# Block-turned loads of x and context, context mask and norm as rows, and one accumulating VectorE operation per head for causal mask, sign and maximum

## The chip, the cores and the metric

The kernel runs on one core of one Trainium2 chip. The metric is the device time of one execution in microseconds (us). All data is fp32 unless said otherwise. The engines are TensorE (PE), ScalarE (ACT), VectorE (DVE), GpSimd (POOL) and SyncE (SP), which here only issues transfers.

## What is computed

The reference chains four blocks over 128 batch rows of 128 x 256. Cut to what matters here:

```python
# block 0: decoder layer, 16 heads of 16, x and context (128, 128, 256)
def _mha(x, kv, Wq, Wk, Wv, mask, causal):
    Q, K, V = (einsum('bsd,hdk->bhsk', t, W) * mask for t, W in ((x, Wq), (kv, Wk), (kv, Wv)))
    energy = einsum('bhsk,bhtk->bhst', Q, K)
    lengths = sum(energy[:, :, 0, :] != 0, axis=-1)      # keys beyond it are masked
    ...                                                  # causal mask for self
    return softmax(energy / sqrt(dk)) @ V * mask
mask0 = 1.0 - all(x == 0, axis=2, keepdims=True)
x1 = layernorm(x + mha(x, x, ..., mask0, causal=True), ln1)
mask1 = 1.0 - all(x1 == 0, axis=2, keepdims=True)
x2 = layernorm(x1 + mha(x1, context, ..., mask1, causal=False), ln2)
x3 = layernorm(x2 + ffn(x2) * mask0, ln3)
# block 1: features = context, query = x3
norm_X = layernorm(context) * n1_w + n1_b;  norm_F = layernorm(x3) * n2_w + n2_b
cross = fc2(gelu(fc1(attention(norm_F, norm_X, norm_X, D ** -0.5))))
norm_cross = layernorm(cross) * n3_w + n3_b
x4 = norm_F + gamma2 * (cross + gamma1 * attention(norm_cross, norm_cross, norm_cross, D ** -0.5))
# block 2
x5 = x4 + softmax(x4 @ context.T) @ context
# block 3: layer norm, 8 heads of 32 on (x5, context), layer norm, projection to u, then
s = silu(s @ A.T) + u_t            # 128 steps in sequence, all batch rows at once
return x6 + states @ C + mod
```

## The kernel before, in words

The 128 batch rows form 64 groups (NG) of G = 2. A group's data is a tile of 128 positions x (2 x 256), called natural, or its transpose of 128 of the 256 features x (2 halves x 256 columns, W), called turned. Ten units carry a group from its input to the store: self_in, self_att, ctx_in, ctx_att (block 0's attentions), ffn, pair (block 1), real (block 2), mix_in, mix_att, mix_out (block 3). After the last group a second part of the program runs the 128 scan steps and writes the output.

Each engine has one list of steps, written out in PROGRAM (lines 139 to 207) as unit.step@lag. The function drive (249 to 260) walks the list once per iteration and runs each step for group i - lag; with a largest lag of 6 there are 70 iterations. An engine works in order, so a step that waits holds up all that stands behind it. The waits are counted semaphores: Steps.done is for a result, Steps.before for a buffer to be free, and BANKS (209 to 223) assigns each matmul result one of eight PSUM banks. At iteration PREPARED (3) each engine also runs a piece of one-time preparation; at MOD_STORED (6) SP stores the rows of mod.

The steps that the change touches:

- self_in.xT, ctx_in.cT, pair.CT and real.ccT on PE turn the natural x, masked context (CB), normalised context (HC) and plain context (CC): four 128x128 matmuls against ident each (L554). ACT copies each result to SBUF (evac, L909; HCT for CT). ctx_in.k and .v, and pair.sc1, mix_in.k and .v, and real.screal consume them.
- ctx_in.amax and keep on DVE (L1198, L1204) find the rows of x1 that aren't all zero; POOL's ctx_in.mask (L1514) multiplies the natural context CB by keep. POOL copies the small keep tiles onward (keep, copies1, copies2), so that the next group may overwrite them.
- lnC: DVE's bn_stats, POOL's power and product give scale and shift per row; ACT's lnC (L988) writes HC from CC; then CT and HCT; DVE's NXT applies n1_w and n1_b out of PSUM.
- self_in.v and ctx_in.v are copied from PSUM by ACT; DVE's valid, copy and vp multiply them by the valid column, which has come from nz, count and spread on DVE and the length matmul on PE.
- ctx_att.x1r on ACT copies x1 (L960), because the next group's ln1 overwrites it.
- self_att.mask.br on DVE adds the causal table to a PSUM tile of four heads (128 x 512, L1120), self_att.max.br takes the negated maximum per head (L1127), and ACT's exp uses it as bias, one piece of 128x128 per head. There are 8 tiles per group.
- softmax_one (pair's two, real's one): maximum (mx), a scaling by -scale (nm), exp with that bias.
- SP's list loads x twice (X for the turn, XR for the residual), context twice (CB, CC), the mod rows, and stores u and the result.

Of the kernel before, what the change touches and what calls it, by code (L numbers as in the profile page):

```python
# [24 lines left out]
G = 2  # L25
# [85 lines left out]
def latest(*counts):  # L111

    high = {}
    for c in counts:
# [26 lines left out]
        ctx_att.scores.10@4 mix_att.scores.00@6 pair.cross@5 ctx_att.values.03@4 ctx_att.values.01@4  # L141
        ctx_att.turn.11@4 ctx_att.values.00@4 ctx_att.values.02@4 ctx_att.turn.12@4 ctx_att.turn.13@4
        ctx_att.turn.10@4 mix_in.k@5 real.ccT@5 ctx_att.values.12@4 ctx_att.values.13@4 ctx_att.values.10@4
        ctx_att.values.11@4 ctx_in.x1T@3 ctx_att.back.0@4 mix_att.turn.02@6 ctx_att.back.1@4 self_att.scores.00@2
        self_att.scores.02@2 self_att.scores.01@2 ctx_in.cT@3 pair.ncT@5 ctx_in.q@3 pair.sc2@5 mix_att.turn.03@6
        ctx_in.k@3 pair.pT2@5 mix_att.turn.00@6 self_att.scores.10@2 self_att.scores.11@2 self_att.scores.03@2
        pair.av@5 mix_att.turn.01@6 self_att.turn.01@2 ffn.x2T@4 mix_att.values.00@6 mix_att.values.03@6
        mix_att.values.01@6 ctx_in.e0@3 mix_att.values.02@6 ffn.fc1@4 self_att.turn.02@2 self_att.turn.00@2
        real.x4T@5 ffn.fc2@4 self_in.len@2 real.screal@5 mix_out.o@6 self_in.xT@1 self_att.turn.03@2
        self_att.turn.11@2 real.pTreal@5 ctx_att.scores.01@3 self_att.scores.13@2 self_att.scores.12@2  # L150
        self_att.values.01@2 self_att.values.02@2 self_att.values.00@2 self_att.values.03@2 real.av@5 ctx_in.v@3
        self_in.k@1 self_att.back.0@2 self_in.q@1 self_att.turn.12@2 self_att.turn.10@2 mix_out.h6T@6
        self_att.turn.13@2 ctx_att.scores.00@3 ctx_att.scores.03@3 ctx_att.scores.02@3 self_in.v@1 ctx_in.len@3
        pair.CT@4 self_att.values.10@2 self_att.values.11@2 self_att.values.13@2 self_att.values.12@2
        ctx_att.scores.11@3 ctx_att.scores.13@3 ctx_att.scores.12@3 real.h5T@5 pair.FT@4 ctx_att.turn.01@3
        mix_in.v@4 pair.sc1@4 self_att.back.1@2 ctx_att.turn.00@3 mix_in.q@5 ctx_att.turn.02@3 ctx_att.turn.03@3
        pair.pT1@4 self_in.e0@1 mix_out.u@6 pair.av1@4
    """,
    "act": """
# [1575 lines left out]
```

## Time and profile before

| | us |
|---|---|
| median of three runs | 4111.22 |
| the runs | 4104.85 to 4113.52 |
| span of the profiled execution | 4106.6 |

The page gives the span of one profiled execution, busy time of each engine in it, and groups of instructions by line, engine and tiles. PE is TensorE's matmuls, PEld its weight loads, which overlap them. A matmul's record overlaps that of the one behind it, so the time that a step takes of an engine is read from its start to the next one's start. Waiting isn't counted as busy.

### The profile page before, as it was taken

Reading aid. Unit: us, or ns where it says so; the run is one execution under the profiler, and the core shown is the slowest. Engines: PE = TensorE matmul, PEld = TensorE weight load, DVE = VectorE, ACT = ScalarE, POOL = GpSimd, SP = SyncE. Lnnn points to the kernel's source line nnn. Section 1 sums busy time; section 2 is a strip of 40 time slices with the busy share of each in tenths; the row PEclk is TensorE's granted clock in tenths of the full one; section 3 lists DMA queues with packets and bytes.
Section 4 is the critical chain, followed back from the end, with each engine's and each line's share of the span. In section 5 each row is a group of like instructions: output and inputs, shape, how many; then the busy total and the mean of one; then the engine's idle time right before and its main releaser. Section 6 shows DMA issues by size and latency. Waiting matters only on the chain. (4 is left out here: it accounts for less than half of the span.)

```text
span 4106.6 us, 111739 instructions
## 1 busy us (share of the span) xinstructions
PE 3913.2 (95%) x37177; PEld 3233.6 (79%) x37177; DVE 3349.2 (82%) x9519; ACT 3547.9 (86%) x8460; POOL 2854.5 (70%) x3172
## 2 busy tenths in 40 slices
PE   6899999999999999999999999999999999999859
PEld 5688888888888888888888888888888888887647
DVE  4788888888888888888888888888888888888635
ACT  4799999999998999999899999989999998999635
POOL 2577777777777777777777777777777777777636
PEclk7999999999999999999999999999999999999969
DMA  3001011011101101110110111011011101100038
GB/s 115 22 29 34 20 31 34 20 34 31 34 20 31 34 21 33 31 34 20 31 34 23 31 31 34 20 31 34 23 32 31 34 20 31 34 24 28 18 80 306
DMA packets 121876, 159.94 MB, mean 39 GB/s; under 512 B 12296, under 2 KB 108450, under 8 KB 116642
## 3 DMA queue, kind: packets, MB, share of 16 engines
q1 hardware_dynamic: 116896, 145.39, 11.5%
q10 hardware_dynamic: 4416, 7.41, 0.5%
q8 instruction: 307, 5.03, 0.5%
q14 instruction: 257, 2.11, 0.2%
HBM read 114.86 MB, written 37.75 MB: 37 GB/s over the span
## 5 line engine op out<-in xcount | busy, mean ns | idle before, releaser
L618 PE MATMUL bank<-ident,prob 128*128 128x128 f32 x5120 | 728.8, 277 | 56.9 <-ACT CR L1005 26.9
L938 ACT ACTIVATE probT<-bank 128x512 f32<-128x512 f32 x1280 | 730.6, 593 | 59.6 <-PE bank L618 56.7
L909 ACT ACTIVATE turned<-bank 128x512 f32<-128x512 f32 x896 | 538.7, 601 | 186.9 <-PE bank L554 177.8
L618 PEld LDWEIGHTS bank<-ident,prob 128*128 128x128 f32 x5120 | 590.9, 142 | 138.4 <-issue 48.8
L1138 DVE TENSOR_REDUCE mx<-bank 128x4 f32<-128x512 f32 x768 | 507.9, 682 | 187.3 <-PE bank L589 184.7
L927 ACT ACTIVATE prob<-prob,mx 128x128 f32<-128x128 f32 x2048 | 650.6, 396 | 4.1 <-DVE mx L1127 4.0
L562 PE MATMUL bank<-turned,shared 128*128 128x256 f32 x2560 | 616.4, 384 | 1.2 <-ACT turned L909 1.1
L1444 POOL TENSOR_TENSOR rs_ln<-ve_ln,half 128x2 f32<-128x2 f32 x320 | 227.3, 710 | 446.8 <-DVE ve_ln L1109 446.8
L1149 DVE TENSOR_TENSOR prob<-bank,mx 128x512 f32<-128x512 f32 x768 | 520.7, 685 | 15.3 <-PE bank L618 1.9
L562 PEld LDWEIGHTS bank<-turned,shared 128*128 128x128 f32 x2560 | 469.8, 191 | 69.0 <-issue 12.3
L919 ACT ACTIVATE prob<-prob 128x512 f32<-128x512 f32 x768 | 475.5, 636 | 13.0 <-DVE prob L1149 12.1
L589 PE MATMUL bank<-shared,turned 32*128 32x256 f32 x4096 | 448.5, 403 | 3.4 <-DVE prob L1120 2.2
L1523 POOL TENSOR_SCALAR shared<-turned,half_of 128x512 f32<-128x512 f32 x256 | 399.7, 1574 | 29.8 <-ACT turned L909 29.7
L1120 DVE TENSOR_TENSOR prob<-bank,causal 128x512 f32<-128x512 f32 x512 | 345.1, 685 | 57.0 <-PE bank L618 47.3
L570 PE MATMUL bank<-shared,turned 128*128 128x256 f32 x1536 | 369.9, 384 | 0.6 <-DVE turned L1256 0.5
L1127 DVE TENSOR_REDUCE mx<-prob 128x4 f32<-128x512 f32 x512 | 347.3, 679 | 16.8
L589 PEld LDWEIGHTS bank<-shared,turned 32*128 32x128 f32 x4096 | 284.7, 185 | 82.6 <-issue 47.2
L570 PEld LDWEIGHTS bank<-shared,turned 128*128 128x128 f32 x1536 | 281.5, 190 | 55.2 <-issue 22.2
L652 PE MATMUL bank<-probT,shared 128*32 128x128 f32 x8192 | 291.7, 278 | 0.9 <-ACT probT L938 0.8
L1458 POOL TENSOR_TENSOR X<-X,row_ln_g 128x512 f32<-128x512 f32 x192 | 245.5, 1279 | 63.2 <-ACT X L988 63.2
L1534 POOL TENSOR_TENSOR prob<-prob,inv 128x512 f32<-128x512 f32 x256 | 263.5, 1040 | 16.7 <-DVE inv L1165 16.7
L652 PEld LDWEIGHTS bank<-probT,shared 128*32 128x32 f32 x8192 | 205.2, 110 | 76.6 <-issue 75.4
(238 smaller groups left out, 9071.8 us busy)
## 6 DMA issues: line engine op xcount, KB each, us to landing
shared<-in_x SPq DMA_DIRECT2D x128, 256.0 KB, 2.9
CB<-in_ctx SPq DMA_DIRECT2D x64, 256.0 KB, 4.0
CC<-in_ctx SPq DMA_DIRECT2D x64, 256.0 KB, 2.7
mod<-mod_rows SPq DMA_DIRECT2D x64, 256.0 KB, 3.8
residual<-X SPq DMA_DIRECT2D x64, 256.0 KB, 3.1
out<-turned SPq DMA_DIRECT2D x16, 1024.0 KB, 4.8
turned<-residual SPq DMA_DIRECT2D x14, 1024.0 KB, 7.1
u_turned<-us SPq DMA_DIRECT2D x124, 32.0 KB, 2.2
```

The costliest lines, as they stand in the source:

```text
L562: last = nc.tensor.matmul(t[:, m * W:(m + 1) * W], w[:, a, m * 128:(m + 1) * 128], src[:, a, :], start=(a == 0), stop=(a == DH - 1))
L570: last = nc.tensor.matmul(t[:, b * D:(b + 1) * D], src[:, a, b * S:(b + 1) * S], w[:, a, :], start=(a == 0), stop=(a == DH - 1))
L589: last = nc.tensor.matmul(t[:, a * W:(a + 1) * W], QT[p][rows_, a, b * S:(b + 1) * S], KEYS[p][rows_, a, :, b * S:(b + 1) * S], start=True ...
L618: last = nc.tensor.transpose(t[:, h * 128:(h + 1) * 128], src[:, h, :], ident[:])
L652: last = nc.tensor.matmul(t[k * 32:(k + 1) * 32, r * 128:(r + 1) * 128], VP[p][:, b, 4 * r + k, :], src[:, k, :], start=True, stop=True)
L909: nc.scalar.activation(dst, banks.of(f"{unit}.{name}")[:, 0:n], ACT.Copy).then_inc(*st["act"].mark(name))
L919: nc.scalar.activation(flat(t), flat(t), ACT.Exp, scale=SCALE[p]).then_inc(*st["act"].mark(f"exp.{b}{r}"))
L927: last = nc.scalar.activation(t[:, h, :], t[:, h, :], ACT.Exp, bias=low[:, h:h + 1], scale=1.0)
L938: nc.scalar.activation(flat(t), banks.of(f"{att}.turn.{b}{r}")[:, :], ACT.Copy).then_inc(*st["act"].mark(f"probT.{b}{r}"))
L1138: nc.vector.tensor_reduce(m[:], banks.of(f"{att}.tile.{b}{r}")[:, :].rearrange("p (h t) -> p h t", h=4), AX, ALU.max)\
L1149: nc.vector.tensor_tensor(t[:], banks.of(f"{att}.tile.{b}{r}")[:, :].rearrange("p (h t) -> p h t", h=4), maxes.of(f"{att}.max.{b}{r}")[:]. ...
L1523: last = nc.gpsimd.tensor_scalar(KEYS[p][:, :, c, :], KT[p][:], half_of[:, c:c + 1], None, ALU.mult)
```

## The change

- x and context are also loaded in blocks: in_blocks issues four DMAs per 256 KB, by an index that swaps 32x32 blocks (runs of 32 elements). A DVE transpose of 128x512, which turns each 32x32 block in place, then gives XT (self_in.xT on DVE) and ccT (ctx_in.cT on DVE, three buffers). The PE steps xT, cT, ccT and CT and the ACT copies behind them go.
- Scaling by position, which in the turned layout is along the row: keep of ctx is stored to HBM (rowout) and loaded back broadcast to all partitions (rowin) as kept_row; lnC's scale and shift likewise as norm_row. POOL computes CBT = ccT * kept_row (mask), HCT = ccT * norm_row 0 (hcs), + norm_row 1 (HCT). ACT's lnC and HCT go; NXT reads HCT in SBUF.
- Causal mask, sign and maximum: per head one tensor_tensor_reduce on DVE writes -(score + causal) and accumulates its minimum; exp has scale -1.
- nz accumulates the count itself; the length matmul takes the count broadcast and the table head_at; valid goes straight into vp's column; vp reads v out of PSUM. nm, count, spread and the ACT copies of v and x1 go, the last by two x1 buffers; keep0 and keep1 get four buffers each in place of POOL's copies.
- New lists and banks, PREPARED 2, MOD_STORED 5; SP's mod load one iteration earlier. The amax of self reads XR.

```diff
-PREPARED, MOD_STORED = 3, 6
+PREPARED, MOD_STORED = 2, 5
...
+    x_q, ctx_q = (t.rearrange("(g b) (k c) (a j i) -> g j c a b k i", b=G, c=32, j=4, i=32) for t in (x_d, ctx_d))
...
+                def in_blocks(t, src, g, here):
+                    v = t[:].rearrange("p b d -> p (b d)").rearrange("p (a b k i) -> p a b k i", a=DH, b=G, i=32)
+                    for j in range(4):
+                        sp.dma_start(v[32 * j:32 * j + 32], src[g, j]).then_inc(here.sem, 16)
...
+                def kept_to(g):
+                    for w in latest(kept_in.before(g), ctx_in["dve"].done("keep", g)):
                         sp.wait_ge(*w)
+                    sp.dma_start(kept_d.rearrange("(b s o) -> s b o", b=G, o=1), keep1[g % 4][:].unsqueeze(2), allow_slow_non_contiguous=True)\
+                        .then_inc(kept_out.sem, 16)
+
+                def kept_from(g):
+                    for w in latest(kept_out.done(g), ctx_in["pool"].before("mask", g)):
+                        sp.wait_ge(*w)
+                    sp.dma_start(kept_row, kept_d.partition_broadcast(128)).then_inc(kept_in.sem, 16)
...
                     def mask_(g):
...
-                        nc.vector.tensor_tensor(t[:], banks.of(f"{att}.tile.{b}{r}")[:, :].rearrange("p (h t) -> p h t", h=4),
-                                                causal[:].unsqueeze(1).to_broadcast([128, 4, 128]), ALU.add).then_inc(*st["dve"].mark(f"mask.{b}{r}"))
-
-                    def low(g):
...
-                        nc.vector.tensor_reduce(m[:], probs.of(f"{att}.mask.{b}{r}")[:], AX, ALU.max, negate=True)\
-                            .then_inc(*st["dve"].mark(f"max.{b}{r}"))
+                        for h in range(4):
+                            last = nc.vector.tensor_tensor_reduce(t[:, h, :], banks.of(f"{att}.tile.{b}{r}")[:, h * 128:(h + 1) * 128], causal[:],
+                                                                  -1.0, 3.0e38, ALU.add, ALU.min, m[:, h:h + 1])
...
+                def x_turned(g):
+                    waits_apart(dve, prep, *latest(x_in.done(g), *(self_in["pe"].before(n, g) for n in "qkv")))
+                    nc.vector.transpose(flat(trn["XT"]), x_blocks.rearrange("p b d -> p (b d)")).then_inc(*self_in["dve"].mark("xT"))
...
                 def mask(g):
 
-                    waits_apart(pool, prep, *latest(ctx_in2.done(g), ctx_in["dve"].done("keep", g)))
-                    for b in range(G):
-                        last = nc.gpsimd.tensor_scalar(nat["CB"][:, b, :], nat["CB"][:, b, :], keep1[0][:, b:b + 1], None, ALU.mult)
-                    last.then_inc(*ctx_in["pool"].mark("mask"))
+                    for w in latest(kept_in.done(g), ctx_in["dve"].done("cT", g), ctx_in["pe"].before("k", g), ctx_in["pe"].before("v", g)):
+                        pool.wait_ge(*w)
+                    nc.gpsimd.tensor_tensor(trn["CBT"][:], ccT[g % 3], kept_row.unsqueeze(1).to_broadcast([128, DH, W]), ALU.mult)\
+                        .then_inc(*ctx_in["pool"].mark("mask"))
```

In PE's new list 17 steps stand between ctx_in.x1T and ctx_in.k:

```
ctx_in.x1T@3 ctx_att.turn.10@4 ctx_att.values.03@4 ctx_att.values.11@4 ctx_att.values.12@4 ctx_att.values.13@4
ctx_att.values.10@4 mix_att.turn.02@6 ctx_att.back.0@4 ctx_att.back.1@4 ctx_in.q@3 pair.ncT@5 self_att.scores.03@2
self_att.scores.01@2 self_att.scores.00@2 mix_att.turn.03@6 pair.sc2@5 mix_att.turn.00@6 ctx_in.k@3
```

SP's new list:

```diff
-        mix_out.load@6 ctx_in.load@3 pair.load@4 self_in.load@0 mix_out.store@6 mix_out.store_u@6 self_att.load@1
+        pair.rowin@4 pair.load@2 self_in.load@0 ctx_in.load@2 ctx_in.rowout@2 mix_out.load@5 mix_out.store@6
+        pair.rowout@3 ctx_in.rowin@2 self_att.load@1 mix_out.store_u@6
```

## Rows read from the trace of the kernel before

**Rows 1.** The page's head: the span and the instructions.

```profile
span 4106.6 us, 111739 instructions
```

**Rows 2.** Line L965 (mix_out.attT, once per group): ns min/median/max, first and last start.

```profile
L965 ACT ACTIVATE turned<-bank x64: 575/598/606, 154.5 to 3916.8; 128x512 f32<-128x512 f32 x64
```

**Rows 3.** Stretch 2000-2060: length, busy PE, PEld, DVE, ACT, POOL, PEclk, DMA, GB/s.

```profile
2000.00:2060.00 60.00, 58.52 (x565) 48.50 (x564) 50.70 (x144) 54.15 (x129) 43.52 (x49) 1.00 0.10 29
```

**Rows 4.** Waits of PE over the whole span: us in total, times, longest.

```profile
PE bank L770 <- ACT y5T L998: 31.0, 64, 1.6
PE bank L618 <- ACT CR L1005: 26.9, 62, 0.5
...
PE bank L618 <- ACT prob L919: 15.4, 64, 1.4
```

**Rows 5.** Timeline of PE: start us, record us, line, result<-operands, matmuls.

```profile
2006.49 0.63 PE L554 MATMUL bank<-ident,HC 128*128 128x128 f32 x4
2007.05 1.08 PE L652 MATMUL bank<-probT,shared 128*32 128x128 f32 x32
...
2027.64 0.60 PE L554 MATMUL bank<-ident,CC 128*128 128x128 f32 x4
2028.17 1.08 PE L652 MATMUL bank<-probT,shared 128*32 128x128 f32 x32
...
2032.60 0.66 PE L554 MATMUL bank<-ident,CB 128*128 128x128 f32 x4
2033.10 0.63 PE L554 MATMUL bank<-ident,NC 128*128 128x128 f32 x4
2033.57 1.89 PE L562 MATMUL bank<-turned,shared 128*128 128x256 f32 x8
...
2051.62 0.60 PE L554 MATMUL bank<-ident,shared 128*128 128x128 f32 x4
2052.06 1.04 PE L618 MATMUL bank<-ident,prob 128*128 128x128 f32 x8
```

**Rows 6.** Groups of ACT by line and shape: busy us, mean ns, idle before.

```profile
L909 ACT ACTIVATE turned<-bank 128x512 f32<-128x512 f32 x896 | 538.7, 601 | 186.9 <-PE bank L554 177.8
...
L988 ACT ACTIVATE HC<-CC,nmr_lnC,rs_lnC 128x256 f32<-128x256 f32 x128 | 70.1, 606 | 0.0
```

**Rows 7.** Timeline of DVE: start us, record us, what.

```profile
2025.74 0.17 DVE L1204 TENSOR_SCALAR keep<-amax_ctx 128x2 f32<-128x2 f32 x1
...
2043.10 0.68 DVE L1120 TENSOR_TENSOR prob<-bank,causal 128x512 f32<-128x512 f32 x1
2043.70 0.67 DVE L1127 TENSOR_REDUCE mx<-prob 128x4 f32<-128x512 f32 x1
2044.29 0.28 DVE L1221 TENSOR_SCALAR nz_ctx<-bank 128x128 f32<-128x128 f32 x1
```

**Rows 8.** Timeline of POOL, with the idle time before it in brackets.

```profile
2023.55 1.29 POOL L1464 TENSOR_TENSOR X<-X,row_ln_b 128x512 f32<-128x512 f32 x1
...
2027.54 1.83 POOL L1514 TENSOR_SCALAR CB<-CB,keep 128x256 f32<-128x256 f32 x2 [1.30 <-issue]
```

**Rows 9.** DMA: queue's packets, MB, share; issues: KB each, us to landing.

```profile
q1 hardware_dynamic: 116896, 145.39, 11.5%
...
shared<-in_x SPq DMA_DIRECT2D x128, 256.0 KB, 2.9
...
mod<-mod_rows SPq DMA_DIRECT2D x64, 256.0 KB, 3.8
...
u_turned<-us SPq DMA_DIRECT2D x124, 32.0 KB, 2.2
```

**Rows 10.** Timeline of SP's queue: start us, us of the issue.

```profile
2021.07 0.47 SPq L497 DMA_DIRECT2D mod<-mod_rows  x1
```

**Rows 11.** Timeline of PE in the first groups: preparation and the next transposes.

```profile
58.15 1.84 PE L818 MATMUL bank<-col_be,w_q 128*128 128x1 f32 x8 [3.45 <-DVE NC L1353]
...
77.58 1.09 PE L554 MATMUL bank<-ident,X 128*128 128x128 f32 x4 [0.56 <-issue]
```

More of the change, by code:

```diff
@@ L140 @@
     "pe": """
[L141 to L155, printed above, removed]
@@ new lines @@
+        mix_att.turn.03@6 pair.sc2@5 mix_att.turn.00@6 ctx_in.k@3 pair.pT2@5 self_att.scores.10@2
+        self_att.scores.02@2 self_att.scores.11@2 mix_att.turn.01@6 pair.av@5 self_att.turn.01@2 self_in.len@2
+        ffn.x2T@4 mix_att.values.03@6 mix_att.values.00@6 mix_att.values.02@6 ctx_in.e0@3 mix_att.values.01@6
+        self_att.turn.00@2 ffn.fc1@4 self_in.v@2 ffn.fc2@4 real.x4T@5 self_att.turn.03@2 self_att.turn.02@2
+        ctx_in.len@3 real.screal@5 mix_out.o@6 self_att.scores.12@2 ctx_att.scores.01@3 self_att.scores.13@2
@@ L162 @@
-        ctx_att.probT.03@4 ctx_att.probT.02@4 pair.gelu@5 self_att.ln1@3 pair.cross@5 ctx_att.exp.13@4
-        ctx_att.exp.10@4 ctx_att.probT.11@4 mix_att.exp.02@6 ctx_att.probT.13@4 ctx_att.probT.12@4
-        ctx_att.probT.10@4 mix_att.exp.03@6 ctx_att.outT.0@4 pair.lnN@5 ctx_att.outT.1@4 real.ccT@5 mix_att.exp.00@6
-        ctx_in.x1T@3 ctx_in.cT@3 mix_att.exp.01@6 pair.ncT@5 mix_att.probT.02@6 self_att.exp.01@2 ctx_in.q@3
-        pair.exp2@5 ctx_att.ln2@4 pair.pT2@5 mix_att.probT.03@6 ctx_in.k@3 mix_att.probT.00@6 self_att.exp.00@2
@@ L199 @@
[L199 to L202 removed]
+        self_att.add@3 pair.lnCpow@4 self_att.ln1pow@3 self_att.ln1nmr@3 ffn.biased@4 real.x5b@6 pair.lnCnmr@4
@@ new lines @@
+        self_att.ln1gain@3 self_att.ln1@3 pair.lnNpow@5 pair.lnNnmr@5 mix_att.part.02@6 pair.lnNgain@5
+        pair.lnN@5 mix_att.part.03@6 ctx_att.add@4 mix_att.part.00@6 ctx_in.mask@3 ctx_att.ln2pow@4
+        ctx_att.ln2nmr@4 mix_att.part.01@6 ctx_att.ln2gain@4 ctx_att.ln2@4 pair.hcs@4 pair.skip@5 pair.gam2@5
+        ffn.x2b@4 pair.x4@5 ctx_in.keys@3 ffn.ln3pow@4 ffn.ln3nmr@4 pair.HCT@4 ffn.ln3gain@4 ffn.ln3@4
+        mix_out.ln6pow@6 mix_out.ln6nmr@6 pair.lnFpow@4 pair.lnFnmr@4 real.ln5pow@5 real.ln5nmr@5 pair.lnFgain@4
@@ new lines @@
+    mix_in.k:0 ctx_att.out.1:0 ctx_in.x1T:6 ctx_att.back.0:1 mix_att.turn.02:2 ctx_att.back.1:7
+    self_att.tile.00:1 self_att.tile.02:5 self_att.tile.01:5 pair.ncT:2 ctx_in.q:6 pair.sc2:4 mix_att.turn.03:3
+    ctx_in.k:3 pair.pT2:4 mix_att.turn.00:6 self_att.tile.10:2 self_att.tile.11:0 self_att.tile.03:7 pair.av:7
+    mix_att.turn.01:1 self_att.turn.01:4 ffn.x2T:5 mix_att.out.0:3 ctx_in.e0:6 ffn.fc1:5 self_att.turn.02:2
+    self_att.turn.00:7 real.x4T:4 ffn.fc2:6 self_in.len:1 self_in.v:3 real.screal:0 mix_out.o:5
@@ L223 @@
+    ctx_att.turn.02:6 ctx_att.turn.03:0 pair.pT1:2 self_in.e0:5 mix_out.u:2 pair.av1:7
 """.split())
```

410 lines of the change are left out of this document (200 added, 210 removed).

## The prediction

> **What bounds the kernel now.** I read the head of the page first: the span is 4106.6 us [rows 1]. Then a view of how one work step recurs, the starts of the 64 mix_out.attT copies: 154.5 to 3916.8 us, so 63 periods of 59.72 us, with about 155 us before and 190 us behind them [rows 2]. Nearly all of the time is 64 repetitions of one pattern, and each microsecond saved or added per group is worth 63 to 64 us. The stretch 2000 to 2060 us, one period, shows which engine is full: TensorE (PE) busy 58.52 of 60.00 us, ScalarE (ACT) 54.15, VectorE (DVE) 50.70, GpSimd (POOL) 43.52, DMA a tenth, TensorE's granted clock 1.00 throughout [rows 3]. So PE's in-order list sets the period; its idle is 1.48 us. The table of waits says what that idle is: the three entries that recur some 62 to 64 times are all waits on ACT, 31.0 + 26.9 + 15.4 = 73.3 us [rows 4]. What counts of an edit is therefore PE time removed, or a wait that PE gains.
>
> Against its own time: the span is 4106.6, the median of the runs 4111.2, so 4.6 lies around the span, and I add it at the end.
>
> **The change, part by part.**
>
> **Four transposing steps leave PE** (xT, cT, CT, ccT: four 128x128 matmuls each). A pipelined step is priced from its start to the start of the step behind it, not by its record: HC 2006.49 to 2007.05 is 0.56, CC 2027.64 to 2028.17 is 0.53, CB 2032.60 to 2033.10 is 0.50, shared (the self input) 2051.62 to 2052.06 is 0.44 [rows 5]. The sum is 2.03 us per group, 64 x 2.03 = **-130 us**. PE gets nothing in return; the length matmul only changes its operands.
>
> **ACT** loses the copies of these four (CT's is HCT), of the two v, the x1r copy (all 128x512, 0.60) and two lnC pieces of 0.61 [rows 6]: 7 x 0.60 + 2 x 0.61 = 5.4 us, from 54.15 to about 48.7. ACT isn't the bound, so this pays only where PE waits on ACT, at most 73 us [rows 4]. They stand behind pair's gelu, the copies of pair.cross and one exponential; those operations stay, though order and banks around them are new, and an ACT that is a tenth emptier reaches them somewhat earlier. I take a fifth, **-16 us** (0 to -73).
>
> **DVE, mask and maximum.** Per self tile a 128x512 addition and a 128x512 reduction go, 0.60 + 0.59 from start to start, eight tiles: -9.5 us. In come 32 accumulating operations of 128x128, each on a PSUM tile and the causal table. The trace has none of that kind. The nearest row is nz, 128x128 out of PSUM: 0.28; the floor is the smallest operation, 0.17, the ceiling nz plus one such for writing the accumulator, 0.45 [rows 7]. I take 0.28: 9.0 us (5.4 to 14.4).
>
> The Trainium skill, "VectorE: DVE Perf Modes", section "The TRN2 errata — SBUF-src ops pay a fixed extra latency per instruction", speaks against this edit: many small tiles each pay the fixed part, so a tile should have 512 elements or more. Its measured form for fp32 tensor_tensor, (N+151)/0.96 ns, gives as an estimate 0.29 us for 128 columns and 0.69 for 512 (the trace has 0.68 for the mask). By it, four small ones take 1.16 us instead of 2 x 0.69 = 1.38: cutting the tile costs three fixed parts but saves one whole pass. The sum would be 9.3 instead of 9.0. The accumulator write isn't in that form.
>
> **DVE, the rest.** Two transposes of 128x512 come in; no such row exists, and at the 0.60 of a 128x512 pass [rows 7] they are 1.2 us (half to double: 0.6 to 2.4). Out go two counts (taken like nz), and seven small steps (two spreads, three nm, two copies) at 0.17: 1.75, less 0.08 of overlap each, 1.05. DVE becomes 50.70 - 9.5 + 9.0 + 1.2 - 1.05 = 50.4 (46 to 57), still 7 us below PE's 56.5. **0.**
>
> **POOL** loses the mask of CB (1.83 for its two pieces) and gets three 128x512 passes at 1.29 (mask, hcs, HCT) [rows 8]: 43.5 - 1.8 + 3.9 = 45.6, uncounted that four tiny keep copies go. **0** by load.
>
> **Loads in blocks.** x and context are now read in runs of 128 bytes: 2048 runs per 256 KB load, 128 on each of 16 DMA engines. The page's queue has 116896 packets in 11.5% of 16 engines' span, 0.115 x 16 x 4106.6 / 116896 = 65 ns each [rows 9], so 128 x 65 ns = 8.3 us per load against 2.9 now. Each is issued an iteration before its use, with some 20 us or more in hand. That slack is the cover; gone, it would cost what rival E says. **0.** Six more issues for the blocks and five for the rows below, at 0.47 [rows 10], are 5.2 us more on SP's queue, whose transfers take a tenth of the engines' time [rows 3].
>
> **The mask row, the new wait.** keep of ctx no longer scales CB on POOL directly. It goes to HBM, comes back broadcast, POOL multiplies ccT by it, and ctx_in.k on PE waits for that. From ln1's end: amax about 0.7 and keep 0.2 [rows 7]; a store, landing like that of u in 2.2; meanwhile SP, where the row's return stands behind the mod load, the result store and two norm rows, issues these four at 0.47 (1.9, beside the 2.2; the waits among them, for mod and lnCnmr on POOL, stand early enough in POOL's list); the return like the mod rows' broadcast, 3.8 [rows 9, 10]; POOL 1.3 [rows 8]. Together 0.9 + 2.2 + 3.8 + 1.3 = 8.2, with a wait or two between, 8.2 to 8.7. The cover is what PE does between x1T, which starts from the same ln1, and k: five values steps (4 take 1.08: 0.27 each), four turns (two take 1.04: 0.52 each), two backs and ncT (0.5 each), q (1.9) [rows 5], together 1.35 + 2.1 + 1.5 + 1.9 = 6.8, and three score tiles and sc2 behind their own inputs, which bring it to 9 if those inputs are there. So k comes between 0 and 2 us late, 0 to 126 us in all. If it is late, all of PE behind it is: pT2, the self scores, then DVE's masks. I take 0, as the score tiles stand ahead of k in the list and the pipeline can slide the other units into the gap; the bound stays in the range. POOL too stands at the mask until the row is there; ln2 queues behind it, and ffn.x2T for that, some 8 steps after k.
>
> The norm rows for HCT take the same way, but are needed half a period later. **0.**
>
> **Prologue.** PE's preparation (from 58.15) moves one iteration forward. In before it lies 19.4 us ahead of the next transposes of groups [rows 11]. Moved forward it can stand in an otherwise empty iteration (0) or hold the first groups up by as much as it lasts (19.4). I take **+8**, since its loads come no earlier. The last stage with its scan isn't changed: 0.
>
> **Sum:** 4106.6 - 130 - 16 + 8 = 3968.6; with 4.6 around the span **3973 us**, the period 59.72 - 2.03 - 0.25 = 57.4.
>
> **The rivals.**
>
> C, *PE's waits on ACT vanish altogether*: ACT and DVE have gained over 5 and 0.3 us, and the order is new. For it: all recurrent waits are on ACT [rows 4]. Against: each is a short chain (score, exponential, turn) whose own latency doesn't shrink. 4106.6 - 130 - 73 + 8 + 4.6 = 3916.
>
> A, *the mask row through HBM comes late*, the one that ends slower. Place: ctx_in.k on PE, behind ctx_in.mask on POOL, behind the row's return on SP. Price: 63 us per microsecond late. It decides from (4111 - 3973) / 63 = 2.2 us per group. At 3 us, the store and the return each some 1.5 us slower than their rows, 3973 + 189 = 4162. For it: 4-byte elements, a store whose like isn't in the trace, and a queue in order. Against: 0.5 to 2 us is what the rows give at most.
>
> B, *DVE becomes the bound*: with 0.45 for each accumulating operation, DVE works 55.8 us; if half of the 9.3 us stay that it idles now [rows 3], its period is 60.4, 4106.6 + 63 x 0.7 + 8 + 4.6 = 4163. Against: the nz row.
>
> D, *another chain through the in-order lists sets the period*, and PE's freed time turns into waits: about 4115. Against: PE is busy 97.5% of the period, so no other chain is known to be as long.
>
> E, *the block loads don't arrive in time.* Two loads of 128 packets per engine fill a group's 57 us from 0.22 us per packet on, 3.4 times the mean. At 19 times the 2.9 us of the plain load, 55 us each, the period would be 110 us, 7000 us in all. The factor is that of the Trainium skill, same page, section "The three transpose paths", a trap: a plain DMA that transposes by strides is 19 times slower than the transposing DMA path when the destination's innermost stride is large. Here the innermost 32 elements are contiguous on both sides, so it hardly applies; no row shows such a load.
>
> **How the numbers follow.** The forecast has 0.62 (its own range 3925 to 4060: relief beyond a fifth below, k late by up to 1.4 us above), C 0.19, A 0.08, D 0.05, B 0.04, E 0.02. The range 3890 to 4085 takes in C with a prologue that costs nothing, and a k late by up to 1.8 us. About 0.2% is what a measurement of this kernel can tell from no change. Faster: forecast and C, 0.81; same: D, 0.05; slower: A, B, E, 0.14.
>
> **What would show it.** Right: PE shows no transposes of HC, CC, CB and x; the period is near 57.4; k's idle before the step is below 0.5 us, and the recurrent waits are still on ACT. Wrong: an idle of 2 us or more before ctx_in.k, released by POOL (A); an accumulating operation of 0.45 or more with DVE busy 95% of the period (B); DVE's transposes waiting on a DMA (E); PE's busy time near 56 in a period still near 59.7 (D). The accumulating operation's mean, the transposes' mean and the landing time of the kept row show the three estimates directly.

## The result, and the profile after

The changed kernel takes **4578.81 us** in the median (4577.64 to 4583.64), the kernel before 4109.74 in the runs beside it: a ratio of 1.1138 (95% interval 1.112 to 1.1157). The forecast was 3973 in a range of 3890 to 4085, so both the size and the sign were wrong. What happened is rival A, the late mask row, but two and a half times as large as that rival made it (469 us against 189), and with a second loss that no case had.

The head of the page after, span and busy time of each engine (before: [rows 1]):

```profile
span 4577.3 us, 111103 instructions
PE 3924.9 (86%) x36153; PEld 3193.7 (70%) x36153; DVE 3181.0 (69%) x12272; ACT 3268.7 (71%) x7884; POOL 2931.5 (64%) x2980
```

The table of PE's waits (us in total, times, longest) has one new entry that is larger than all of [rows 4] together:

```profile
PE bank L597 <- POOL turned L1500: 433.7, 64, 12.7
```

L597 is the projection step, L1500 ctx_in.mask on POOL. So ctx_in.k waits in every group, 433.7 / 64 = 6.8 us. The view of L1500 itself names who POOL waited for, with total and times:

```profile
  DMA shared<-kept_rows: 466.0, 64
```

That is the row's return. One group, on the timelines of SP's queue, POOL and PE (start us, record us, line, operation, idle before and its releaser in brackets):

```profile
2064.09 0.37 SPq L507 DMA_DIRECT2D kept_rows<-keep  x1
...
2065.55 0.41 SPq L519 DMA_DIRECT2D norm_rows<-rs_lnC  x1
2066.00 0.52 SPq L519 DMA_DIRECT2D norm_rows<-nmr_lnC  x1
2071.56 0.33 SPq L513 DMA_DIRECT2D shared<-kept_rows  x1
...
2078.44 1.26 POOL L1500 TENSOR_TENSOR turned<-shared 128x512 f32<-128x512 f32 x1 [5.97 <-DMA shared<-kept_rows]
...
2079.84 3.75 PE L597 MATMUL bank<-turned,shared 128*128 128x256 f32 x8 [5.71 <-POOL turned L1500]
```

The store of keep is issued at 2064.09. SP issues the four transfers ahead of the row's return, as the prediction had it, in 2.0 us, then stands until 2071.56, since the store has not landed. The return takes another 6.9 us to the mask's start. The step of k then costs 3.75 us where the row of before has 1.89 [rows 5]. The reason is in the granted clock. Three stretches of this group (length; busy PE, PEld, DVE, ACT, POOL with their counts; PEclk; DMA; GB/s):

```profile
2072.00:2080.00 8.00, 2.29 (x20) 1.94 (x18) 5.00 (x36) 1.58 (x6) 2.03 (x3) 0.81 0.25 69
2080.00:2085.00 5.00, 5.00 (x23) 3.55 (x23) 0.00 (x0) 2.02 (x6) 4.55 (x6) 0.62 0.11 35
2085.00:2120.00 35.00, 35.00 (x317) 30.14 (x315) 27.44 (x112) 30.21 (x79) 25.11 (x25) 1.00 0.13 25
```

PE works 2.29 of 8 us, the clock drops from its upper level (1.00, 2.4 GHz) towards the lower one (half, 1.2 GHz), and the 5 us behind the wait run at a mean of 0.62. In the 35 us behind them the clock is whole and PE is full, as in [rows 3].

The parts of the change that the prediction priced with bounds, from DVE's groups (busy us, mean ns | idle before), beside its timeline of one self tile:

```profile
L1134 DVE CUSTOM_DVE_ANT_0 prob<-bank,causal 128x128 f32<-128x128 f32 x2048 | 459.6, 285 | 573.6 <-PE bank L653 543.1 <-PE bank L624 29.6 <-issue 0.8
L1134 DVE DVE_READ_ACCUMULATOR2_ANT mx<- 128x1 f32 x2048 | 169.9, 83 | 0.0
...
L1202 DVE STREAM_TRANSPOSE turned<-shared 128x512 f32<-128x512 f32 x64 | 44.5, 695 | 4.4 <-DMA shared<-in_x 4.4
```

```profile
2087.40 0.28 DVE L1134 CUSTOM_DVE_ANT_0 prob<-bank,causal 128x128 f32<-128x128 f32 x1
2087.61 0.08 DVE L1134 DVE_READ_ACCUMULATOR2_ANT mx<- 128x1 f32 x1
2087.61 0.29 DVE L1134 CUSTOM_DVE_ANT_0 prob<-bank,causal 128x128 f32<-128x128 f32 x1
...
2088.24 0.28 DVE L1245 TENSOR_SCALAR shared<-bank,iota 128x32 f32<-128x32 f32 x1
```

An accumulating operation has a record of 0.28 us and a readout of 0.08, but the next one starts 0.21 behind it: a tile's four take 2088.24 - 2087.40 = 0.84 us. The transposes take 0.70.

The block loads, from the DMA issues (packets, KB each, median us from issue to landing):

```profile
shared<-in_x SPq DMA_DIRECT2D x256, 64.0 KB, 2.5
CB<-in_ctx SPq DMA_DIRECT2D x256, 64.0 KB, 2.4
```

### The profile page after: what moved, and what is told of

Its sections match the earlier page's. It is cut to its first block and busy times, and to the rows that moved or that the text cites. A ratio compares the mean times of both kernels' runs of the same rounds, so it can differ in the third digit from the quotient of the medians.

```text
span 4577.3 us, 111103 instructions
## 1 busy us (share of the span) xinstructions
PE 3924.9 (86%) x36153; PEld 3193.7 (70%) x36153; DVE 3181.0 (69%) x12272; ACT 3268.7 (71%) x7884; POOL 2931.5 (64%) x2980
## 5 line engine op out<-in xcount | busy, mean ns | idle before, releaser
L597 PE MATMUL bank<-turned,shared 128*128 128x256 f32 x2560 | 732.3, 437 | 454.3 <-POOL turned L1500 433.7
L597 PEld LDWEIGHTS bank<-turned,shared 128*128 128x128 f32 x2560 | 536.4, 219 | 552.7 <-issue 468.4
L1134 DVE CUSTOM_DVE_ANT_0 prob<-bank,causal 128x128 f32<-128x128 f32 x2048 | 459.6, 285 | 573.6 <-PE bank L653 543.1
L653 PE MATMUL bank<-ident,prob 128*128 128x128 f32 x5120 | 770.3, 280 | 38.7 <-ACT probT L964 25.8
L653 PEld LDWEIGHTS bank<-ident,prob 128*128 128x128 f32 x5120 | 579.3, 142 | 195.6 <-issue 73.5
L935 ACT ACTIVATE turned<-bank 128x512 f32<-128x512 f32 x704 | 412.9, 594 | 216.1 <-PE bank L589 174.1
L1005 ACT ACTIVATE X<-Z,nmr_ln,rs_ln 128x256 f32<-128x256 f32 x192 | 104.8, 592 | 418.6 <-POOL nmr_ln L1449 417.8
L1500 POOL TENSOR_TENSOR turned<-shared 128x512 f32<-128x512 f32 x64 | 81.3, 1270 | 466.0 <-DMA shared<-kept_rows 466.0
L605 PE MATMUL bank<-shared,turned 128*128 128x256 f32 x1536 | 354.4, 380 | 2.1 <-DVE turned L1261 2.1
L1459 POOL TENSOR_TENSOR X<-X,row_ln_g 128x512 f32<-128x512 f32 x160 | 203.3, 1270 | 116.5 <-ACT X L1005 116.4
```

Of the source, the lines that this page charges most:

```text
L597: last = nc.tensor.matmul(t[:, m * W:(m + 1) * W], w[:, a, m * 128:(m + 1) * 128], src[:, a, :], start=(a == 0), stop=(a == DH - 1))
L605: last = nc.tensor.matmul(t[:, b * D:(b + 1) * D], src[:, a, b * S:(b + 1) * S], w[:, a, :], start=(a == 0), stop=(a == DH - 1))
L653: last = nc.tensor.transpose(t[:, h * 128:(h + 1) * 128], src[:, h, :], ident[:])
L935: nc.scalar.activation(dst, banks.of(f"{unit}.{name}")[:, 0:n], ACT.Copy, scale=scale).then_inc(*st["act"].mark(name))
L1134: last = nc.vector.tensor_tensor_reduce(t[:, h, :], banks.of(f"{att}.tile.{b}{r}")[:, h * 128:(h + 1) * 128], causal[:], -1.0, 3.0e38, ALU ...
```

## The experiments

Two theories at the start. The **late row**: the mask row, with the clock that its wait costs, is the whole loss, and the rest of the sum stands. The **new order**: the lists stall one another, and the wait at k is only the place where it shows. Each kernel below is the changed one with the edit named.

### The mask row left out

```diff
-        ... ctx_in.load@2 ctx_in.rowout@2 mix_out.load@5 ... pair.rowout@3 ctx_in.rowin@2 self_att.load@1 ...
+        ... ctx_in.load@2 mix_out.load@5 ... pair.rowout@3 self_att.load@1 ...
-   nc.gpsimd.tensor_tensor(trn["CBT"][:], ccT[g % 3], kept_row.unsqueeze(1)..., ALU.mult)
+   nc.gpsimd.tensor_tensor(trn["CBT"][:], ccT[g % 3], ones_row[:].unsqueeze(1)..., ALU.mult)
```

> Left out: the context mask. POOL multiplies the context by a row of ones written once, and keep of ctx no longer goes to HBM and back; all else is as in the changed kernel. Theory L (the late mask row is the whole of the loss): PE's 434 us of waits at ctx_in.k go, and with them the slow clock behind each, which is about 142 us (PE busy 3924.9 us where 3913.2 less the removed 130 would be 3783): 4577 - 434 - 142 = about 4000 us, PE busy near 3790, granted clock 1.00 in mid-kernel. Theory O (the new order of the lists, or DVE, is a bound of its own behind the row): 4060 to 4115, with waits of PE on DVE or ACT of 2 us or more per group.

Measured: 4109.52 us, a ratio to the kernel before of 0.9992 (0.9983 to 1.0002). The spans, 4577.3 - 4108.6, differ by **468.7 us**. By the pages, PE's idle time falls from 4577.3 - 3924.9 = 652.4 to 292.6 us, so 359.8 of it was waiting, and PE's busy time falls by 3924.9 - 3816.0 = 108.9 for the same 36153 matmuls: the lowered clock. By the trace's record of the granted clock, PE is busy at half clock for 355.9 us in the changed kernel and for 157.1 us here; at whole clock half of the difference, 99 us, would not have been spent. But the kernel is then only level with the one before, 136 us above the forecast. The late row isn't the whole loss.

The head of its page, its largest recurrent wait of PE, and the starts of successive u steps on DVE's timeline:

```profile
span 4108.6 us, 110850 instructions
PE 3816.0 (93%) x36153; PEld 3131.2 (76%) x36153; DVE 3217.6 (78%) x12273; ACT 3269.6 (80%) x7884; POOL 2935.3 (71%) x2980
```

```profile
PE bank L701 <- ACT outT L980: 55.4, 31, 3.7
```

```profile
653.50 0.31 DVE L1340 TENSOR_SCALAR us<-bank,u_b 128x128 f32<-128x128 f32 x1
...
712.37 0.31 DVE L1340 TENSOR_SCALAR us<-bank,u_b 128x128 f32<-128x128 f32 x1
...
769.77 0.31 DVE L1340 TENSOR_SCALAR us<-bank,u_b 128x128 f32<-128x128 f32 x1
...
832.84 0.31 DVE L1340 TENSOR_SCALAR us<-bank,u_b 128x128 f32<-128x128 f32 x1
```

The periods are 58.87, 57.40 and 63.07 us. In the middle of the kernel before they lie between 59.4 and 60.3 us; here some groups lose 1.5 to 6 us and others nothing. The time is the one that the new order was expected to give, but its waits of 2 us per group aren't there: 55.4 us over 64 groups are 0.9.

### The mask row by PE instead of HBM

Two matmuls of keep, broadcast along the columns, with the identity put the row in a PSUM bank; DVE multiplies ccT by it. The computation is whole.

```diff
+   for b in range(G):
+       last = nc.tensor.matmul(t[:, b * S:(b + 1) * S], keep1[g % 4][:, b:b + 1].to_broadcast([128, 128]), ident[:], ...)
...
+   nc.vector.tensor_tensor(trn["CBT"][:], ccT[g % 3], banks.of("ctx_in.row")[:, 0:W].unsqueeze(1)..., ALU.mult)
```

> The whole computation; the mask row is made on the chip instead of through HBM: two 128x128 matmuls of keep (broadcast over the stationary columns) against ident give the row in PSUM on all partitions, DVE multiplies ccT by it (128x512), and POOL's mask pass and both transfers of the row go. PE gains about 0.25 us per group, DVE one pass of 0.69 at a place behind norm.1. Theory L: as row_const plus 16 us of PE, 4010 to 4030. Theory O: 4075 to 4130. If DVE's step at that place holds up what is behind it, PE shows waits on DVE at ctx_in.k or at the self scores' turns.

Measured: 4120.54 us; 1.0017 (1.0005 to 1.0029). A row that never leaves the core costs some 11 us more than no row at all, and the same 136 us and more remain: they don't hang on the mask.

### The return directly behind its store

```diff
-        ... ctx_in.load@2 ctx_in.rowout@2 mix_out.load@5 mix_out.store@6 pair.rowout@3 ctx_in.rowin@2 ...
+        ... ctx_in.load@2 ctx_in.rowout@2 ctx_in.rowin@2 mix_out.load@5 mix_out.store@6 pair.rowout@3 ...
```

> Only SP's list differs: the return of the mask row stands directly behind its store, ahead of the mod load, the result store and the two norm rows. In the changed kernel the store takes 8.7 us from issue to the return's issue, the return 6.8 to POOL's pass. Theory E (256 elements of 4 bytes make the store slow by themselves): the store stays above 7 us, since the first group had 7.3 with neither mod nor result store in flight; the return falls to about 4, as it is no longer behind the norm rows' 512 elements; PE waits some 3 us instead of 7: about 4320 us. Theory T (the traffic between makes it slow): store 2 to 4 us, return 4, no wait at k worth naming: about 4000 to 4030.

Measured: 4686.19 us; 1.1398 (1.1371 to 1.1426). It was expected near 4320, so this is a miss, but it tells two things. With nothing issued behind the store, it still took 8.24 us in the median from its issue to the return's, against 8.62 in the changed kernel: what makes it slow isn't the traffic issued behind it. And while the return itself came faster (5.1 us in the mean to the mask's start, where it was 6.8), the norm rows are now issued later, and POOL stands for them:

```profile
PE bank L597 <- POOL turned L1500: 305.0, 64, 8.9
PE bank L589 <- POOL X L1552: 155.2, 62, 5.2
```

```profile
POOL turned L1507 <- DMA shared<-norm_rows: 389.2, 63, 8.1
POOL turned L1500 <- DMA shared<-kept_rows: 336.0, 64, 14.9
```

The first fence is PE's waits, the second POOL's. The wait at k shrinks by 129 us, a new one of 155 comes up at the transposing of x4 (L1552). The norm rows, "needed half a period later", have no such slack once SP's queue holds them back. Most of the miss is again the clock: against the changed kernel PE is idle for only 27 us more (4693.6 - 4014.0 = 679.6 against 652.4) but busy for 89 us more, and busy at half clock for 521.1 us instead of 355.9, which is worth 83 of them.

### The mask row stored in runs of 128 bytes

keep is 128 x 2; turned in 32x32 blocks by DVE (0.2 us), its values lie along the free axis, and 8 runs of 128 bytes replace 256 elements of 4 bytes. The turn is a step of its own on DVE, behind keep. SP's order is the changed kernel's.

```diff
-   sp.dma_start(kept_d.rearrange("(b s o) -> s b o", b=G, o=1), keep1[g % 4][:].unsqueeze(2), allow_slow_non_contiguous=True)
+   nc.vector.transpose(keep1_t[:], keep1_w[g % 4][:])
+   for b in range(G):
+       sp.dma_start(kept_d.rearrange("(b j c) -> b j c", b=G, c=32)[b], keep1_t[b:128:32, :])
```

> Only the form of the store differs: DVE turns the two keep columns in 32x32 blocks (one more instruction of some 0.2 us), and two transfers store 8 runs of 128 bytes instead of 256 elements of 4 bytes; SP's list is as in the changed kernel. Theory E: from the store's issue to the return's issue 2.5 to 4 us instead of 8.7; the return stays near 6.8 behind the norm rows' stores; PE waits 1 to 3 us: 4080 to 4250. Theory T: 8 us or more as before, about 4570.

Measured: 4452.76 us; 1.0831 (1.0809 to 1.0852). SP's queue in one group:

```profile
2061.83 1.14 SPq L511 DMA_DIRECT2D kept_rows<-keep_t  x2
...
2064.48 0.51 SPq L522 DMA_DIRECT2D norm_rows<-nmr_lnC  x1
2065.09 0.49 SPq L516 DMA_DIRECT2D shared<-kept_rows  x1
...
2074.35 0.34 SPq L528 DMA_DIRECT2D shared<-norm_rows  x1
```

In the same order beside the same traffic, SP issues the return at once behind the norm rows: the store's two halves have landed by then, 3.26 us behind the issue of the first (2065.09 - 2061.83) and, in the median over the groups, 2.66 behind that of the second, where it was 8.62; in SP's waits there is no entry for this store any more. **The store's 8.6 us are its 256 elements** (the turned row also lies in 8 partitions instead of 128; the two aren't told apart). But the return now takes 9.7 us to the mask in the mean instead of 6.8, with the norm rows' 512 elements ahead of it, and PE still waits 304.6 us at k. That these elements are the reason shows further down: with both rows in runs the return takes 3.7.

### Both rows left out

The scaling and addition of the norm rows go against a row of ones too, so the computation lacks mask and normalisation; the POOL passes stay.

```diff
-   nc.gpsimd.tensor_tensor(trn["HCT"][:], ccT[g % 3], norm_row[:, 0, :].unsqueeze(1)..., ALU.mult)
+   nc.gpsimd.tensor_tensor(trn["HCT"][:], ccT[g % 3], ones_row[:].unsqueeze(1)..., ALU.mult)
-   nc.gpsimd.tensor_tensor(trn["HCT"][:], trn["HCT"][:], norm_row[:, 1, :].unsqueeze(1)..., ALU.add)
+   nc.gpsimd.tensor_tensor(trn["HCT"][:], trn["HCT"][:], ones_row[:].unsqueeze(1)..., ALU.add)
```

> Left out: the context mask and the norm of the context (both rows are ones, written once), so that no row goes through HBM. row_const still had the norm rows. There the period, seen between the u steps, swings from 57.1 to 63.5 us; the short ones are the 57.4 that was forecast, the long ones have one stall of up to 3.8 us at PE's back.1, in which PE, ACT, DVE and POOL stand together while an instruction packet of 8 KB takes 3.8 us on its DMA engine; 30 of 367 such packets take over 2 us, in the kernel before none. Theory I (the norm rows' 512 elements of 4 bytes hold the DMA engines for some 10 us per group, and the engines' instructions come late behind them): without them no packet over 2 us, the period 57.4 throughout, 64 x 1.7 = about 110 us less than row_const's 4109: about 4000. Theory D (the new lists' own order makes the swing, instruction packets are a companion): the swing stays, 4080 to 4110.

Measured: 3988.13 us; 0.9706 (0.969 to 0.9722): **121.4 us** below the kernel without the mask row (118 by the two ratios to the kernel before), 15 above the forecast. The head of its page:

```profile
span 3985.3 us, 110468 instructions
PE 3770.2 (95%) x36153; PEld 3099.6 (78%) x36153; DVE 3206.3 (80%) x12273; ACT 3260.5 (82%) x7884; POOL 2930.6 (74%) x2980
```

The spans differ by 4108.6 - 3985.3 = 123.3 us: 292.6 - 215.1 = 77.5 are idle time of PE, 66.5 of them before the matmuls of one line, L701, and 3816.0 - 3770.2 = 45.8 are slower matmuls (busy at half clock for 157.1 us with the norm rows, for 65.3 without). Its u steps:

```profile
631.99 0.31 DVE L1340 TENSOR_SCALAR us<-bank,u_b 128x128 f32<-128x128 f32 x1
...
689.57 0.31 DVE L1340 TENSOR_SCALAR us<-bank,u_b 128x128 f32<-128x128 f32 x1
...
746.96 0.31 DVE L1340 TENSOR_SCALAR us<-bank,u_b 128x128 f32<-128x128 f32 x1
```

57.58 and 57.39: steady, at the forecast's 57.4. So the norm rows cost some 2 us per group, although POOL's waits in the kernel without the mask row have no entry for them. Where, is seen in that kernel in a group that lost time (timelines of PE, ACT and DVE):

```profile
784.15 1.12 PE L701 MATMUL bank<-ident,outT 128*128 128x128 f32 x4 [3.48 <-ACT outT L980]
783.50 0.60 ACT L980 ACTIVATE outT<-bank 128x512 f32<-128x512 f32 x1 [3.32 <-remote]
783.55 0.26 DVE L1185 RECIPROCAL recip_ctx<-bank 128x16 f32<-128x16 f32 x1 [2.60 <-remote]
```

PE, ACT and DVE stand together, and ACT and DVE for "remote", which is no engine of the core. The DMA queues between 779 and 785 us (packets, MB, share of 16 engines):

```profile
q1 hardware_dynamic: 207, 0.24, 40.2%
q14 instruction: 1, 0.01, 3.9%
```

One packet of instructions held its DMA engine for 0.039 x 16 x 6 = 3.7 us. Counted over the instruction packets of 8 and 16 KB between 1000 and 3500 us: over 2 us took none of 362 in the kernel before (longest 1.5), 30 of 367 without the mask row (longest 8.3), none of 375 without both rows. So the elements reach past their own transfer: with them, packets of other queues come late.

That the late instructions make the stalls doesn't follow, though. Of the first 58 periods of the kernel without the mask row, the 29 with an instruction packet of over 2 us and the 29 without one both take 59.3 us in the mean. Of the 26 times between 600 and 3500 us that PE is idle for over 0.8 us, 13 have an instruction packet of over 1 us under way, as in the group above, and 13 have none. What they share is place and time: 24 stand before L701, and 25 begin between the issue of the norm rows' store and that of their return; without both rows there is no such idle time at all. The stalls come with the elements, then; by what way isn't shown.

### Both rows in runs of 128 bytes

The edit of the mask row, and the same for the norm rows: rs and nmr of lnC side by side in one tile, turned by DVE, 16 runs instead of 512 elements. The computation is whole.

```diff
+   rs["lnC"] = lnc_w[:, 0:G]
+   nmr["lnC"] = lnc_w[:, G:2 * G]
+   nc.vector.transpose(lnc_t[:], lnc_w[:])
-   sp.dma_start(norm_d[k].rearrange("(b s o) -> s b o", b=G, o=1), t[:].unsqueeze(2), allow_slow_non_contiguous=True)
+   sp.dma_start(norm_d[k].rearrange("(b j c) -> b j c", b=G, c=32)[b], lnc_t[G * k + b:128:32, :])
```

> The whole computation. Both rows still go through HBM, in SP's order of the changed kernel, but DVE first turns keep and the norm's columns in 32x32 blocks, and the stores are runs of 128 bytes: 8 runs for the mask, 16 for the norm rows, in place of 768 elements of 4 bytes per group. In row_wide (mask alone) the store fell from 8.7 to 2.7 us, but the return grew to 9.8 behind the norm rows' elements. Theory I with E (elements of 4 bytes are the whole cost): store 2.7, return about 4.5, pass 1.3 = 8.5 after the store's issue, inside the cover of 16.7 - 6.8 = 9.9; PE waits under 1 us at ctx_in.k; about 4000 to 4040. If the round trip stays late for another reason: a wait of 3 us or more, 4200.

Measured: **3999.58 us; 0.9732 (0.9712 to 0.9751)**, and in a second set of runs:

> rows_wide again, as the base of the two kernels beside it, and for its interval: 3999.6 us before, 3990 to 4010 expected.

4004.15 us; 0.9737 (0.9721 to 0.9753). This beats both kernels: 2.6% under the one before, 12.5% under the changed one. The profile of the second set (span 4000.7 us): busy times from the page, PE's largest recurrent wait, SP's queue, and the step of k:

```profile
PE 3792.6 (95%) x36153; PEld 3099.2 (77%) x36153; DVE 3228.7 (81%) x12405; ACT 3270.7 (82%) x7884; POOL 2933.2 (73%) x2980
```

```profile
PE bank L659 <- ACT probT L970: 26.6, 63, 0.7
```

```profile
2027.14 1.14 SPq L514 DMA_DIRECT2D kept_rows<-keep_t  x2
...
2031.49 0.38 SPq L519 DMA_DIRECT2D shared<-kept_rows  x1
...
2084.58 1.14 SPq L514 DMA_DIRECT2D kept_rows<-keep_t  x2
```

```profile
2094.22 1.89 PE L603 MATMUL bank<-turned,shared 128*128 128x256 f32 x8
```

The wait at k is gone (4.4 us in the whole span), k is back at 1.89 us, the period is 57.44, and no instruction packet of 380 takes over 2 us (longest 1.9). The transposes and POOL's mask are all still there, so the new order isn't the cause: with its DMAs in other packets, the same order reaches the forecast's period.

### The mask by PE, the norm rows in runs; the scan's loads moved

The two matmuls of above together with the 16 runs:

> The whole computation: the mask row by PE and DVE as in row_pe, the norm rows through HBM in runs of 128 bytes as in rows_wide. row_pe's mid-kernel period was within 0.1 us of row_const's. Theory I: no instruction packet over 2 us, period near 57.5, about 4005 to 4020. Theory D: 4090 to 4120 as row_pe.

Measured: 4011.33 us; 0.976 (0.9741 to 0.978), which the intervals don't tell apart from the mask row in runs through HBM. And that kernel with the last stage's early loads issued behind the result store of the last group but one instead of ahead of it:

```diff
-                    if g == NG - 1:
-                        scan_early()
...
+                    if g == NG - 2:
+                        scan_early()
```

> pe_wide with one more edit: the early loads for the scan (u and residual, 4 MB and more) are issued behind the second-last group's result store instead of ahead of it. In row_const the store of that group was issued at 3936, right behind those loads, and DVE's res of the last group waited 44 us for it; in the kernel before the store came 37 us after the loads. Expected from this: the last interval between u steps from 62.5 to about 27 as before, 35 us less than pe_wide: 3970 to 3985, where the forecast for the change stood. If the loads' lateness then shows at the scan's start, 10 to 20 us of it come back.

Measured: 4007.53 us; 0.9749 (0.9733 to 0.9766), no measurable gain. In the changed kernel, and in those without rows or with both in runs, DVE stands once for the residual near the end, 44.0 to 44.2 us (here without both rows: waits of DVE); the table of the kernel before has no such entry:

```profile
DVE X L1334 <- DMA residual<-X: 44.1, 1, 44.1
```

With the loads moved, PE stands at the start of the scan instead (waits of PE):

```profile
PE bank L1646 <- POOL Z L1662: 33.6, 1, 33.6
```

So the lateness has moved to another wait of the last stage and isn't gone. What would take it away isn't shown.

### The old mask and maximum, everything else as in the best version

The maximum is a step of its own again, directly behind the addition.

```diff
-   for h in range(4):
-       last = nc.vector.tensor_tensor_reduce(t[:, h, :], ..., causal[:], -1.0, 3.0e38, ALU.add, ALU.min, m[:, h:h + 1])
+   nc.vector.tensor_tensor(t[:], ..., causal[:].unsqueeze(1).to_broadcast([128, 4, 128]), ALU.add)
+   nc.vector.tensor_reduce(m[:], probs.of(f"{att}.mask.{b}{r}")[:], AX, ALU.max, negate=True)
```

> rows_wide with one part of the change undone: mask and maximum of a self tile again by a 128x512 addition and a 128x512 reduction on DVE, exp with scale 1. In the trace of the changed kernel four accumulating operations start 0.21 us apart, 0.83 per tile where the two old ones took 1.19, so DVE gets 8 x 0.36 = 2.9 us more per group, some 53 of 57.5. Theory S (as forecast: DVE's time is hidden, the edit is worth nothing): 3990 to 4010. Theory F (the tile's latency between scores and exp is on the path): up to 64 x 2.9 = 186 us more, 4050 to 4190.

Measured: 4054.21 us; 0.9861 (0.9845 to 0.9877), **50 us** more than the 4004.15 beside it. A recurrent wait of PE that the best version doesn't have, and DVE's group of the mask:

```profile
PE bank L595 <- DVE prob L1138: 31.7, 62, 0.5
```

```profile
L1138 DVE TENSOR_TENSOR prob<-bank,causal 128x512 f32<-128x512 f32 x512 | 347.8, 679 | 5.9 <-PE bank L630 5.9
```

A transposing step (L595) waits once per group for a bank that DVE's mask has yet to read out. DVE is nowhere the bound by load, 84% of this span. The addition by itself (0.68) isn't longer than the four accumulating operations (0.84), but with the reduction of one tile ahead of the addition of the next, banks come free later: two tiles in a row start at 2003.41 and 2004.80, 1.39 us apart, where the kernel before needs 1.19 for the pair. The steps stand in the best version's order, not in the old kernel's, so 50 us is what the edit is worth in this order. By the pages 31.4 of the 50.3 us between the spans are idle time of PE, and 18.9 are busy time for the same matmuls at the same mean clock (0.979); why these take longer is open.

### Four transposing steps of PE done twice

Of x2, NF, NC and x4, 16 matmuls more per group, in the best version: the opposite of the change's main term.

```diff
+   for _ in range(2 if any(src is nat[n] for n in ("X2", "NF", "NC", "X4")) else 1):
        for a in range(DH):
```

> rows_wide with PE work put back: four of the transposing steps that are left (x2T, FT, ncT, x4T) do their four matmuls twice into the same bank, 16 matmuls of 0.11 us more per group, as many as the change took away, with no wait or copy added. Theory P (PE's start-to-start work sets the period, as the sum has it): 64 x 1.76 = 113 us more, 4105 to 4120. Theory C (a chain through ACT and DVE sets it, PE has slack): under 50 us more.

Measured: 4106.02 us; 0.9983 (0.9974 to 0.9993): **102 us** more, of 113 expected. Time put on PE costs 0.9 of its price here; that time taken away is worth as much is inferred from it, not measured.

## Why the prediction was wrong, by its steps

| step | forecast | measured |
|---|---|---|
| four transposing steps leave PE | -130 us | 102 of 113 us for four others put back |
| ACT's relief | -16 | recurrent waits on ACT 73.3 to 26.6 in the best version |
| DVE's mask and maximum | 0 | about -50, in the new order |
| block loads | 0 | 0 (DVE waits once, 4.4 us) |
| prologue | +8 | +11 in the best version |
| last stage | 0 | about +36 in the best version |
| norm rows | 0 | **+121**, measured without the mask row |
| mask row | 0, up to 126 | **+469**, measured beside the norm rows |

**The mask row: the right chain, two terms too small.** The prediction made the chain behind keep 2.2 + 3.8 + 1.3 = 7.3 us. It is 16.7 in the mean. "A store, landing like that of u in 2.2" is the first step that failed: 8.62 in the median, at least 7.29. The row that I took is a store of 32 KB in runs [rows 9]; its 2.2 us say nothing of 256 elements of 4 bytes, and I named these elements in rival A without bounding them. "The return like the mod rows' broadcast, 3.8" is the second: 6.77 in the mean, as it stands behind the norm rows' elements. The cover was slightly larger than taken: 16.7 - 6.8 = 9.9 behind keep, for 6.8 to 9 from x1T on. POOL's pass (1.26, taken 1.29) was right. Against the cover as measured, the true store alone would have made k 4 us late, both 7.

**The price of lateness was too small too.** "63 us per microsecond late" counts only the wait. PE's 6.8 us of standing take the clock along: 359.8 us of idle time and 108.9 us of slower matmuls. Here the clock is a third of the wait on top.

**The norm rows: "0" by slack.** The slack was there for the data; yet with the elements under way PE, ACT and DVE stood together in many groups, at a step that has no need of the rows. The prediction looked at who waits for the rows, not at what else goes on while they are stored. That the 121 us are idle time and slow matmuls behind the stalls at one step is measured (77.5 + 45.8 between the spans), and so is that they go when the rows go in runs. Late instruction packets go with the elements too (13 of 325 over 2 us in the changed kernel, 16 of 338 with the mask row alone in runs; none with both rows in runs or left out), but groups that have them lose no more time than groups that don't (59.3 us a period either way). By what way the elements make the engines stand stays open.

**The main term was about right.** With the elements gone, the period is 57.4 as forecast. The best version's span can be put together from the forecast: the 64 u steps lie 116 us closer together than before. That is 152 us less in the repeating part (forecast 130 + 16 = 146), and 36 us more in the last interval (26.9 to 62.6). The first u step comes 11 us later (forecast 8). Together 106 us, and 4106.6 - 4000.7 is 105.9. But single terms offset each other in the 152: by the run with steps doubled the four steps are worth about 130 x 102 / 113 = 117, by the run with the old mask DVE's edit 50, together 167 without ACT's share. What takes the difference back, perhaps POOL's and SP's added work, stays open.

**DVE: "0" because it isn't the bound.** The size was slightly wrong (0.84 us per tile where 4 x 0.28 = 1.12 was taken, against 1.19 of the old pair). The reason for nothing was wrong: an engine 7 us below the bound still decides when a bank comes free for PE. The Trainium skill, "VectorE: DVE Perf Modes", section "The TRN2 errata — SBUF-src ops pay a fixed extra latency per instruction", would have had four small tiles pay their fixed part four times; the trace shows the next one starting 0.21 us behind the last, 0.08 less than the estimate of 0.29 by the page's form, so a part of it overlaps here.

**The last stage: "isn't changed: 0".** Its code isn't, but its first loads are issued among the last groups by SP's list, which is new. How they could be hidden stays open.

**The rivals.** A was the mechanism with a chance of 0.08; its "3 us late, 4162" should have had 7 us and the clock. B and E are refuted: DVE is 81% busy in the best version, and a block load's 64 KB quarter lands in 2.4 to 2.5 us. E's 55 us also multiplied the plain load by a factor that the prediction itself quotes against the transposing path. C's vanishing waits came in part, without the gain. D's 4115 is close to what the kernels without the mask row took (4109.52 and 4120.54), but not by its mechanism: the same lists reach 57.4 us once the elements are gone. The ledger from forecast to result is 3973 + 469 (mask row and clock) + 121 (norm rows) + 15 (the rest as of the run without both rows) = 4578, by its making.

The shares in it depend on the order in which the rows are mended, since the norm rows' elements also hold up the mask row's return. Taken out of the mask row first, the elements are worth 4578.81 - 4452.76 = 126 us, and those of the norm rows then 4452.76 - 4004.15 = 449. The mask row by itself, with the norm rows in runs, was not run. What is shown is that the elements of both rows together are the loss.

## What to carry to other kernels

Before a small row is sent through HBM, ask in how many pieces it goes, not how many bytes it has: the same 1 KB took 8.6 us in 4-byte elements and some 3.3 or less in eight runs, and a 32x32 turn of 0.2 us on VectorE is all that lies between. A transfer that nobody waits for can still cost time; so look for stalls in which all engines stand together, and at periods that swing, and take the transfer out to see whether they go. Put two such transfers right together before judging either: mending one of them gave 126 us here, mending both 575. And price a wait of the bounding TensorE with the clock that falls behind it.

## What the hardware showed that I had not expected

- A store of 256 elements of 4 bytes: 8.62 us from issue to the return's issue beside other traffic, 8.24 with none issued behind it. Reading in runs of 128 bytes is another matter: 151552 such packets (1000 to 3500 us in the changed kernel) took 13 ns each in the mean, where I had taken 65.
- While the elements are under way the DMA engines are busy and move next to nothing. Between 2068 and 2072 us in the changed kernel, by the view of DMA (packets; the queue's share of 16 engines), 522 of 581 packets are under 512 bytes and 83.1% of the engines' time brings 0.06 MB:

```profile
DMA packets 581, 0.08 MB, mean 19 GB/s; under 512 B 522, under 2 KB 580, under 8 KB 580
...
q1 hardware_dynamic: 580, 0.06, 83.1%
```

  The records of 4-byte packets are short (9 ns in the median; the best version, which stores no such elements, still has some 12100 of the 40320 that lie between 1000 and 3500 us here), but 47 of them took over 1 us, up to 4.5, and packets of other transfers beside them up to 5.8. The Trainium skill, "DMA: Bandwidth & Descriptors", section "Specifications", has the line rate from 512 bytes on and a read, change and write below. A slow store fits that for 4 bytes; for stores in 128-byte runs, also below, the runs show no such delay (landed within some 3.3 us). Why the one and not the other isn't shown.
- Accumulating VectorE operations of 128x128 out of PSUM follow each other every 0.21 us with records of 0.28, their readouts (0.08) wholly inside.
- TensorE at half clock for a step (3.75 against 1.89 us) behind a wait of 5.7 us; over the 64 groups the step of k took 2.87 to 3.75, median 3.75.
